# Two groups of columns per cycle, with one stretch of 64-row tiles, in a Fourier mixing layer

## The chip, the cores and the metric

The kernel runs on one core of one Trainium2 chip. The metric is the device time of one execution in microseconds (us). The kernel before takes 5095.11 us, the median of three runs (5094.22 to 5102.17).

## What is computed

x is 4 images of 128 x 128 pixels with 768 channels in 8 blocks of 96. All in float32:

```
xf = rfft2(x, axes=(1, 2), norm='ortho')          # 128 x 65 frequencies, complex
o1 = relu(xf @ w1[block] + b1)                    # complex product, relu on both parts
o2 = o1 @ w2[block] + b2                          # complex product
o  = softshrink(o2, 0.01)                         # on both parts
out = irfft2(o, s=(128, 128), norm='ortho') + x
```

## The kernel before

**Units and stages.** One unit is one image and one block of 96 channels; there are 32 units, and x of two units lies in SBUF (`xs[0]`, `xs[1]`, index `par`). For a unit n, TensorE (PE) does stage A (transform along the width, 24 groups of 4 rows, L760), the layers, and the inverse (E, L849, and F, L859 to L861). Two of the 24 A groups of unit n+1 (`AHEAD`) come between the layers and the inverse of unit n, the others behind the inverse. ScalarE (ACT) and VectorE (DVE) copy A's results into `spectrum` (U), split E's results into two parts, and add F's results to x.

**The layers.** They go through 17 groups s of up to four column frequencies (`GROUPS`; group 2, `REAL`, has two, the last has three). Stage B is the transform along the height's channels times w1: `stage_b_whole` (L778, 128-row tiles) and `stage_b_halved` (L790), where two tiles of 64 rows, y = 0 and y = 1, lie in the upper and the lower half of PE's rows. Stage C (L807) is the transform along the height. Stage D is the product with w2: `stage_d_outer` (L822, 128 rows) and `stage_d_middle` (L832, 64-row tiles). One full fp32 matmul shows as two records, so a full group has 8 records in each of L778, L790, L822 and L832 and 12 in L807.

**Who does what between them.** ACT gathers a group's columns out of U into `whole` (L493, L494) and `halved` (L495, L496), which have two buffers each, `s % 2`. DVE copies B's result to `mixed` (L655). ACT applies bias and relu to C's outer tiles, giving `hidden` (L530, L533), and DVE to the middle tile, giving `middle` (L668). DVE writes b2 into D's banks ahead (the seed, L678). ACT computes `excess` (L524) and DVE the softshrink (L663). B is in PSUM banks 0 and 1, C in 2 and 3, D in 4, 5 for even groups and 6, 7 for odd ones. Group REAL goes through `real_kw` and the flip, two matmuls at L839 and L840, copied to U by ACT (L536).

**Order.** Each engine runs its own list in program order; semaphores are the only ties. PE's cycle s (L864) is: whole of s, outer and middle of s-2, halved of s, C of s-1. So the 64-row tiles of middle and halved form one stretch per group. DVE's cycle (L645) is: mixed(s), shrink(s-2), middle(s-1), seed(s), then in cycles 2 to 9 one `unfold_step` of the unit before (two for each of four pieces of x, each about a quarter of the rows), and in cycles 10 to 15 one `prepare_step` (sign changes of the next unit's weights, L611 and L615; the first waits for these weights).

**x and the weights.** When both unfold steps of a piece are done, SyncE's queue (SP) stores the piece (L392). Its order is: store piece 0, load the next unit's weights (L367), store piece 1, load piece 0 of the unit after next (L387), store 2, load 1, store 3, load 2, load 3. GpSimd (POOL) folds each loaded piece in two steps (L439 to L445), and stage A waits for the fold of its piece.

Of the kernel before, what the change touches and what calls it, by code (L numbers as in the profile page):

```python
# [1 line left out]

# [7 lines left out]
ALU = mybir.AluOpType  # L10
# [17 lines left out]
REAL = 2  # L28

# [130 lines left out]
def fourier_mlp(nc, x, w1, b1, w2, b2, dft, out):  # L160
    with ExitStack() as ctx:
# [60 lines left out]
        def banks_b(s):  # L222

            return 6 if s == 1 else 0
# [15 lines left out]
        bank_c = bank(2).rearrange("p (y i h) -> p y i h", y=2, i=2)  # L240
        middle_c = bank(3, SIZE, 2 * SIZE).rearrange("p (i h) -> p i h", i=2)
# [51 lines left out]
        b_done, b_copied = sem("b_done"), sem("b_copied")  # L293
# [175 lines left out]
        def _(act):  # L469
            def gather(s):  # L470
                w, h, first = whole[s % 2], halved[s % 2], GROUPS[s][0]
                if s == REAL:
                    re, im = (U[:, :, j:j + 2].rearrange("p s k -> p k s") for j in (2, SIZE + 2))
                    act.activation(w[0:BLOCK, :, :, 0], re[0:BLOCK], ACT.Copy)
                    act.activation(w[BLOCK:SIZE, :, :, 0], im[HALF:BLOCK], ACT.Copy).then_inc(whole_gathered, 1)
                    act.activation(h[0:HALF, :, 0], im[0:HALF, 0], ACT.Copy)
                    act.activation(h[HALF:SIZE, :, 0], im[0:HALF, 1], ACT.Copy).then_inc(halved_gathered, 1)
                    return
# [5 lines left out]
                if GROUPS[s][3] is None:  # L484
# [3 lines left out]
                    act.activation(w[BLOCK:SIZE, 1, :, 0], U[HALF:BLOCK, :, j + 5], ACT.Copy).then_inc(whole_gathered, 1)  # L488
                    act.activation(h[0:HALF], U[0:HALF, :, j + 2:j + 4], ACT.Copy)
# [3 lines left out]
                act.activation(w[0:BLOCK], parts[0:BLOCK, 0], ACT.Copy)  # L493
                act.activation(w[BLOCK:SIZE], parts[HALF:BLOCK, 1], ACT.Copy).then_inc(whole_gathered, 1)  # L494
# [3 lines left out]
            def forward(n):  # L498
                for at in A_ACT:
# [4 lines left out]
                    act.activation(third, src[BLOCK:], ACT.Copy).then_inc(act_copied, 1)  # L504
            def layers(m, par, n):
# [4 lines left out]
                gather(0)  # L510
                act.wait_ge(w_loaded[par], (m + 1) * W_LOADS * 16)
                for s in range(NS + 2):
                    if s + 1 < NS:
                        if s >= 1:
                            act.wait_ge(b_done, n * NS + s)
                        gather(s + 1)

                    for stage in ("sums", "tiles") if s < NS else ("tiles", "sums"):
                        if stage == "sums" and s >= 2:
                            t = s - 2  # L520
                            act.wait_ge(d_done, n * NS + (t + 1))
                            if t >= 1:
                                act.wait_ge(shrunk, n * NS + t)
                            act.activation(excess[:, :, 0:rows_d(t)], parts_d(t), ACT.Relu,  # L524
                                           bias=over[:, 0:1]).then_inc(excess_done, 1)
                        if stage == "tiles" and 1 <= s <= NS:
                            t = s - 1
                            act.wait_ge(c_done, n * NS + (t + 1))
                            tiles = hidden[t % 2]
                            act.activation(tiles[:, 0, 0:pairs(t)], bank_c[:, 0, 0:pairs(t)], ACT.Relu,  # L530
                                           bias=b1t[par][:, 0:1]).then_inc(relu_done, 1)
                            k = pairs(t) if None not in GROUPS[t] else 1
                            act.activation(tiles[:, 1, 0:k], bank_c[:, 1, 0:k], ACT.Relu,  # L533
                                           bias=b1t[par][:, 2:3]).then_inc(relu_done, 1)
# [27 lines left out]
        def _(dve):  # L562
# [54 lines left out]
            def forward(n):  # L617
# [26 lines left out]
                dve.tensor_copy(halved[0][HALF:SIZE, slice(*INNER)], parts[0:HALF, 1, 1]).then_inc(first_halved, 1)  # L644
            def layers(m, par, n, first, last):  # L645
                for s in range(NS + 2):
                    if s < NS:
                        k = pairs(s)
                        dve.wait_ge(b_done, n * NS + (s + 1))
                        if s == 1:  # L650
                            for i in range(2):
                                flat = mixed[s % 2][:, i].rearrange("p y (r o) -> p y r o", r=2)
                                copied = dve.tensor_copy(flat, both_b(s, i))
                        else:
                            copied = dve.tensor_copy(mixed[s % 2][:, 0:k], both_b(s)[:, 0:k])  # L655
                        copied.then_inc(b_copied, 1)
                    for stage in ("sums", "tiles") if s < NS else ("tiles", "sums"):
                        if stage == "sums" and s >= 2:
                            t, rows = s - 2, rows_d(s - 2)
                            j = 2 + 2 * GROUPS[t][0]  # L660
                            dst = real_kw[:, :, :] if t == REAL else U[:, 0:BLOCK, j:j + rows]
                            dve.wait_ge(excess_done, n * NS + (t + 1))
                            dve.scalar_tensor_tensor(dst, parts_d(t), LAMBDA, excess[:, :, 0:rows], op0=ALU.add,  # L663
                                                     op1=ALU.min).then_inc(shrunk, 1)
                        if stage == "tiles" and 1 <= s <= NS:
                            t = s - 1
                            dve.wait_ge(c_done, n * NS + (t + 1))
                            dve.tensor_scalar(middle[t % 2][:, 0:pairs(t)], middle_c[:, 0:pairs(t)], b1t[par][:, 1:2], 0.0,  # L668
                                              ALU.add, ALU.max).then_inc(middle_done, 1)
                    if s < NS:  # L670


                        k = rows_d(s) // 2
                        if s == 1:
                            dve.wait_ge(b_copied, n * NS + 2)
                        elif s >= 2:
                            dve.wait_ge(shrunk, n * NS + (s - 1))
                        dve.tensor_copy(bank_d(s).rearrange("p (k r) c -> p k r c", r=2)[:, 0:k],  # L678
                                        b2_rows[par][:, :, :].unsqueeze(1).broadcast_to([SIZE, k, 2, BLOCK])).then_inc(seeded, 1)

                    if 2 <= s < 2 + 2 * NP and not first:
                        unfold_step(n - 1, 1 - par, s - 2)

                    if 2 + 2 * NP <= s < 2 + 2 * NP + W_SIGNS and not last:
                        prepare_step(m + par, 1 - par, s - 2 - 2 * NP)
# [244 lines left out]
```

## Time and profile before

| what | value |
|---|---|
| time of the profiled execution | 5094.22 us, span 5094.2 us |
| median of three | 5095.11 us |
| PE busy | 4981.3 us, 98% |
| DVE busy | 3816.7 us, 75% |
| ACT busy | 2996.3 us, 59% |
| POOL busy | 1436.3 us, 28% |
| mean granted TensorE clock | 0.993 |
| DMA | 430.24 MB, mean 84 GB/s |

The span runs from the first to the last instruction. Matmul records overlap, since the next one starts while the last one's results are still leaving the array; what one block of matmuls costs is therefore read from the start of its first record to the start of the next block's first record. A unit takes 5094.2 / 32 = 159 us.

### The profile page before, as it was taken

To read this page: it belongs to the slowest core of one execution; us is meant where nothing else is said; L and a number is where in the kernel's file an instruction comes from. 1 tells how busy PE (TensorE), PEld (TensorE's weight loads), DVE (VectorE), ACT (ScalarE), POOL (GpSimd) and SP (SyncE) were. 2 spreads that over 40 slices of the span, in tenths; PEclk is the share of its full clock that TensorE was granted. 3 is DMA by queue.
4 is the path that set the end of the run, shared out by engine and by line. 5 is a ranking of instruction groups with operands and counts; after the bars stand their busy time and mean duration, and the time that the engine had idled before them with its cause. 6 is when DMAs were issued, how large, how long until landed. Compare 5 with 4: busy or idle time off the path is not lost.

```text
span 5094.2 us, 113221 instructions
## 1 busy us (share of the span) xinstructions
PE 4981.3 (98%) x40000; PEld 4673.3 (92%) x40000; DVE 3816.7 (75%) x6159; ACT 2996.3 (59%) x5409; POOL 1436.3 (28%) x905
## 2 busy tenths in 40 slices
PE   6999999999999999999999999999999999999997
PEld 6999999999999999999999999999999999999996
DVE  5777777777777777777777777777777777777876
ACT  4555655556655566555566555665556655556653
POOL 3033223332123332233321333312333123332220
PEclk8999999999999999999999999999999999999998
DMA  5044423444323443234442344432344323444233
GB/s 114 12 94 105 98 59 69 91 105 105 68 57 87 105 105 87 56 81 94 105 105 52 70 90 105 106 70 62 79 105 106 86 61 78 92 105 105 61 73 72
DMA packets 1699712, 430.24 MB, mean 84 GB/s; under 512 B 1698848, under 2 KB 1698976, under 8 KB 1699104
## 3 DMA queue, kind: packets, MB, share of 16 engines
q1 hardware_dynamic: 1696768, 421.83, 37.5%
q8 instruction: 346, 5.67, 0.5%
q14 instruction: 262, 2.15, 0.1%
q10 hardware_dynamic: 2336, 0.59, 0.1%
HBM read 220.84 MB, written 201.33 MB: 83 GB/s over the span
## 4 chain that ended last, share of the span: by engine, by line
PE 96%; DVE 2%; issue 1%; SPq 1%; ACT 0%; DMA 0%; DVEq 0%; ACTq 0%
PE psum L807 15%; PE psum L778 14%; PE psum L822 14%; PE psum L760 13%; PE psum L849 13%; PE psum L832 9%; PE psum L790 7%; PE psum L859 3%; PE psum L860 3%; PE psum L861 3%; DVE mixed L655 1%; SPq L387 1%; DVE spectrum L628 0%; PE psum L840 0%; PE psum L839 0%
## 5 line engine op out<-in xcount | busy, mean ns | idle before, releaser
L655 DVE COPY mixed<-psum 128x768 f32<-128x768 f32 (+1 forms) x512 | 477.4, 932 | 700.0 <-PE psum L790 700.0
L541 ACT ACTIVATE sums_high<-psum 128x512 fp32r<-128x512 f32 x768 | 459.2, 599 | 731.3 <-PE psum L849 731.2
L807 PEld LDWEIGHTS psum<-mats,mixed 128*128 128x128 f32 x6272 | 744.0, 191 | 121.2 <-issue 113.1
L807 PE MATMUL psum<-mats,mixed 128*128 128x128 f32 x6272 | 841.8, 283 | 0.0
L778 PE MATMUL psum<-w_whole,whole 128*128 128x192 f32 x4160 | 782.3, 330 | 40.9 <-ACT whole L482 11.4
L822 PE MATMUL psum<-w2t,hidden 128*128 128x192 f32 x4160 | 771.7, 328 | 0.0
L849 PE MATMUL psum<-mats,spectrum 128*128 128x128 f32 x6144 | 743.7, 275 | 3.1 <-DVE spectrum L663 1.6
L760 PE MATMUL psum<-mats,x 128*128 128x128 f32 x6144 | 704.9, 277 | 33.6 <-DVE x L582 17.8
L760 PEld LDWEIGHTS psum<-mats,x 128*128 128x128 f32 x6144 | 696.0, 193 | 40.9 <-issue 23.0
L778 PEld LDWEIGHTS psum<-w_whole,whole 128*128 128x128 f32 x4160 | 673.3, 197 | 60.6 <-issue 33.7
L849 PEld LDWEIGHTS psum<-mats,spectrum 128*128 128x128 f32 x6144 | 714.5, 192 | 4.1 <-DVE sums_low L701 2.0
L701 DVE TENSOR_TENSOR sums_low<-psum,sums_high 128x512 fp32r<-128x512 f32 x768 | 530.4, 691 | 248.8 <-ACT sums_high L541 248.7
L822 PEld LDWEIGHTS psum<-w2t,hidden 128*128 128x128 f32 x4160 | 685.9, 190 | 13.4 <-issue 7.2
L524 ACT ACTIVATE excess<-psum,over 128x768 f32<-128x768 f32 (+1 forms) x544 | 481.8, 886 | 332.8 <-PE psum L832 329.9
L530 ACT ACTIVATE hidden<-psum,b1t 128x256 f32<-128x256 f32 (+1 forms) x544 | 254.6, 468 | 688.8 <-PE psum L807 688.8
L453 POOL TENSOR_TENSOR x<-x,half 128x3072 f32<-128x3072 f32 x32 | 169.8, 5307 | 1450.0 <-DVE halved L644 1450.0
L663 DVE SCALAR_TENSOR_TENSOR spectrum<-psum,excess 128x768 f32<-128x768 f32 (+1 forms) x512 | 480.8, 939 | 118.7 <-ACT excess L524 113.0
L678 DVE COPY psum<-b_rows 128x768 f32<-128x768 f32 (+1 forms) x544 | 504.0, 926 | 0.0
L436 POOL TENSOR_TENSOR x<-x 128x192 f32<-128x192 f32 x31 | 15.7, 505 | 1700.4 <-DMA x<-x 1700.4
L832 PE MATMUL psum<-w2t,middle 64*128 64x192 f32 x4160 | 490.3, 350 | 0.0
L859 PE MATMUL psum<-sums_high,iw_high 128*128 128x260 f32 (+1 forms) x1536 | 461.8, 301 | 0.0
L445 POOL TENSOR_TENSOR x<-x,doubled 128x640 f32<-128x640 f32 (+1 forms) x248 | 443.4, 1788 | 17.0
(76 smaller groups left out, 7800.7 us busy)
## 6 DMA issues: line engine op xcount, KB each, us to landing
x<-x SPq DMA_DIRECT2D x736, 192.0 KB, 2.9
out<-x SPq DMA_DIRECT2D x736, 192.0 KB, 2.5
x<-x SPq DMA_DIRECT2D x736, 64.0 KB, 2.6
out<-x SPq DMA_DIRECT2D x736, 64.0 KB, 2.2
x<-x SPq DMA_DIRECT2D x32, 144.0 KB, 2.7
out<-x SPq DMA_DIRECT2D x32, 144.0 KB, 2.3
w2t<-L_conv_w SPq DMA_DIRECT2D x124, 36.0 KB, 1.8
x<-x SPq DMA_DIRECT2D x64, 48.0 KB, 2.4
```

The source lines that it names most:

```text
L524: act.activation(excess[:, :, 0:rows_d(t)], parts_d(t), ACT.Relu, bias=over[:, 0:1]).then_inc(excess_done, 1)
L655: copied = dve.tensor_copy(mixed[s % 2][:, 0:k], both_b(s)[:, 0:k])
L663: dve.scalar_tensor_tensor(dst, parts_d(t), LAMBDA, excess[:, :, 0:rows], op0=ALU.add, op1=ALU.min).then_inc(shrunk, 1)
L678: dve.tensor_copy(bank_d(s).rearrange("p (k r) c -> p k r c", r=2)[:, 0:k], b2_rows[par][:, :, :].unsqueeze(1).broadcast_to([SIZE, k, 2, B ...
L701: dve.tensor_tensor(sums_low[:, q % RING], bank_e(q), sums_high[:, q % RING], ALU.subtract).then_inc(low_copied, 1)
L760: last = pe.matmul(bank_a(at)[:, i * SIZE:(i + 1) * SIZE], xs[par][:, j, :], mat(FW_EVEN if g[0] < NP else FW_ODD), start=i == 0, stop=Tru ...
L778: pe.matmul(bank_b(s, k), whole[s % 2][:, k // 2, :, k % 2], w1_whole[par][:, :, :].rearrange("p r o -> p (r o)"), start=k % 2 == 0, stop= ...
L807: last = pe.matmul(out[tile], flat[:, tile * SIZE:(tile + 1) * SIZE], mat(FH), start=True, stop=True)
L822: pe.matmul(sums_d(s, k), hidden[s % 2][:, k // 2, k % 2], w2_tile(par, slice(0, SIZE), 2 * (k // 2)), start=False, stop=False, skip_group ...
L832: last = pe.matmul(sums_d(s, i + 2 * y), middle[s % 2][rows, i], w2_tile(par, rows, 1), start=False, stop=True, skip_group_check=True)
L849: last = pe.matmul(bank_e(q)[:, :, i], U[:, q * CHUNK + i, 4:], mat(IH_FIRST if q * CHUNK < THIRD else IH), start=True, stop=True)
L859: pe.matmul(out, iw_high[:, j], high, start=True, stop=False)
```

## The change

PE takes groups in pairs (`PAIRED`: (0, 1), (2, 3), ..., (14, 15), (16)). For a pair (e, o) and the pair before it (e', o'), the cycle is: halved(e), middle(e'), halved(o), middle(o'), whole(e), outer(e'), whole(o), outer(o'), C(e), C(o). All 64-row tiles of the four stages form one stretch. Since halved now comes before whole, halved opens the accumulation (`start`) and whole closes it; in D, middle now opens and outer closes. B and C of an odd group are in banks 2 and 3, of an even one in 0 and 1, and C writes into the banks that B had; so halved(s) waits for the relus and the middle of group s-2. The semaphore `b_done` becomes two, `whole_read` and `halved_read`. For the first pair the two wholes come first, then the two halved, then both C. At the end of the layers one A group of the next unit comes before middle(16), and the flip comes last, followed by the second A group. ACT and DVE follow in the same pairs. DVE's unfold steps are one per pair (cycles 1 to 8), the sign steps two per pair (cycles 5 to 7), between mixed(e) and shrink(e').

```diff
+PAIRED = [tuple(range(s, min(s + 2, NS))) for s in range(0, NS, 2)]
...
-            return 6 if s == 1 else 0
+            return 6 if s == 1 else 2 * (s % 2)
...
-        bank_c = bank(2).rearrange("p (y i h) -> p y i h", y=2, i=2)
-        middle_c = bank(3, SIZE, 2 * SIZE).rearrange("p (i h) -> p i h", i=2)
+        def bank_c(s):
+            return bank(2 * (s % 2)).rearrange("p (y i h) -> p y i h", y=2, i=2)
+
+        def middle_c(s):
+            return bank(2 * (s % 2) + 1, SIZE, 2 * SIZE).rearrange("p (i h) -> p i h", i=2)
...
+                gather_whole(1)
+                gather_halved(1)
+                for j, pair in enumerate(PAIRED):
+                    e, o = pair[0], pair[-1]
+                    for s in pair:
+                        if s + 2 < NS:
+                            if j == 0 and s == e:
+                                act.wait_ge(whole_read, n * NS + (s + 1))
+                                gather_whole(s + 2)
+                            act.wait_ge(halved_read, n * NS + (s + 1))
+                            gather_halved(s + 2)
+                    if j > 0:
+                        if o != e:
+                            act.wait_ge(whole_read, n * NS + (o - 1))
+                            gather_whole(o)
+                        exceed(n, PAIRED[j - 1][0])
+                        if e + 2 < NS:
+                            act.wait_ge(whole_read, n * NS + (e + 1))
+                            gather_whole(e + 2)
+                        exceed(n, PAIRED[j - 1][1])
+                    for s in pair:
+                        rectify(par, n, s)
+                exceed(n, NS - 1)
...
+                for j, pair in enumerate(PAIRED):
+                    e, o = pair[0], pair[-1]
+                    mix(n, e)
+                    for k in range(2 * (j - 5), 2 * (j - 5) + 2):
+                        if 0 <= k < W_SIGNS and not last:
+                            prepare_step(m + par, 1 - par, k)
+                    if j > 0:
+                        shrink(n, PAIRED[j - 1][0])
+                    if o != e:
+                        mix(n, o)
+                    seed(par, n, e)
+                    rectify_middle(par, n, e)
+                    if j > 0:
+                        shrink(n, PAIRED[j - 1][1])
+                    if o != e:
+                        rectify_middle(par, n, o)
+                        seed(par, n, o)
+                    if 1 <= j <= 2 * NP and not first:
+                        unfold_step(n - 1, 1 - par, j - 1)
+                shrink(n, NS - 1)
...
             def stage_c(n, s):
                 pe.wait_ge(b_copied, n * NS + (s + 1))
-                if s == 0:
+                if s == 1:
 
                     pe.wait_ge(f_late_added, n * LATE)
-                if s >= 1:
-                    pe.wait_ge(relu_done, n * (2 * NS) + 2 * s)
-                    pe.wait_ge(middle_done, n * NS + s)
...
+            def layers(par, n, ahead):
+                for s in PAIRED[0]:
+                    stage_b_whole(par, n, s, True)
+                for s in PAIRED[0]:
+                    stage_b_halved(par, n, s, False)
+                for s in PAIRED[0]:
+                    stage_c(n, s)
+                for before, pair in zip(PAIRED, PAIRED[1:]):
+                    for s, t in zip_longest(pair, before):
+                        if s is not None:
+                            stage_b_halved(par, n, s, True)
+                        stage_d_middle(par, n, t)
+                    for s, t in zip_longest(pair, before):
+                        if s is not None:
+                            stage_b_whole(par, n, s, False)
+                        stage_d_outer(par, n, t)
+                    for s in pair:
+                        stage_c(n, s)
+                if ahead:
+                    stage_a(*ahead, 0, 1)
+                stage_d_middle(par, n, NS - 1)
+                stage_d_outer(par, n, NS - 1)
+                flip(n)
+                if ahead:
+                    stage_a(*ahead, 1, AHEAD)
```

PE's list in the middle of the layers of the kernel before, from whole of one group on. `w_whole,whole` is the B whole stage, `w2t,hidden` the outer and `w2t,middle` the middle stage of D, `w_halved,halved` the B halved stage, `mats,mixed` stage C; REGISTER_ALU rows prepare a wait.

```order
L775 REGISTER_ALU
L778 MATMUL psum<-w_whole,whole 128x192 x4
L817 REGISTER_ALU
L822 MATMUL psum<-w2t,hidden 128x2x96 x2
L821 REGISTER_ALU
L822 MATMUL psum<-w2t,hidden 128x2x96 x2
L832 MATMUL psum<-w2t,middle 128x2x96 x4
L785 REGISTER_ALU
L790 MATMUL psum<-w_halved,halved 128x192 x4
L807 MATMUL psum<-mats,mixed 128x128 x6
```

The 64-row rows, L832 and L790, stand together, once per group. The same place in the changed kernel, from halved(e) on:

```order
L839 MATMUL psum<-w_halved,halved 128x192 x4
L870 MATMUL psum<-w2t,middle 128x2x96 x4
L830 REGISTER_ALU
L833 REGISTER_ALU
L839 MATMUL psum<-w_halved,halved 128x192 x4
L870 MATMUL psum<-w2t,middle 128x2x96 x4
L819 REGISTER_ALU
L822 MATMUL psum<-w_whole,whole 128x192 x4
L876 MATMUL psum<-w2t,hidden 128x2x96 x4
L819 REGISTER_ALU
L822 MATMUL psum<-w_whole,whole 128x192 x4
L876 MATMUL psum<-w2t,hidden 128x2x96 x4
```

Halved and middle alternate four times in one stretch, then whole and outer four times; the row behind these is `mats,mixed` x12, the C of both groups. In both kernels every stage has the same number of matmuls per group.

DVE's list of the kernel before, around the first sign steps (L611). What is in brackets is what the row waits for.

```order
L678 COPY psum<-b_rows 128x8x96 [waits shrunk]
L611 TENSOR_SCALAR w_whole<-w_whole 32x96 [waits w_loaded1]
L655 COPY mixed<-psum 128x768 [waits b_done]
L663 SCALAR_TENSOR_TENSOR spectrum<-psum,excess 128x96x8 [waits excess_done]
L668 TENSOR_SCALAR middle<-psum,b1t 128x256 [waits c_done]
L678 COPY psum<-b_rows 128x8x96 [waits shrunk]
L611 TENSOR_SCALAR w_halved<-w_halved 128x96
```

And of the changed kernel, cycle 5 from mixed(e) to the seed of o and on to the next mixed(e):

```order
L686 COPY mixed<-psum 128x768 [waits halved_read,whole_read]
L643 TENSOR_SCALAR w_whole<-w_whole 32x96 [waits w_loaded1]
L643 TENSOR_SCALAR w_halved<-w_halved 128x96
L694 SCALAR_TENSOR_TENSOR spectrum<-psum,excess 128x96x8 [waits excess_done]
L686 COPY mixed<-psum 128x768 [waits halved_read,whole_read]
L708 COPY psum<-b_rows 128x8x96 [waits shrunk]
L699 TENSOR_SCALAR middle<-psum,b1t 128x256 [waits c_done]
L694 SCALAR_TENSOR_TENSOR spectrum<-psum,excess 128x96x8 [waits excess_done]
L699 TENSOR_SCALAR middle<-psum,b1t 128x256 [waits c_done]
L708 COPY psum<-b_rows 128x8x96 [waits shrunk]
L686 COPY mixed<-psum 128x768 [waits halved_read,whole_read]
```

Both first sign steps, with the wait for the weights, now stand between mixed(e) and shrink(e'), ahead of mixed(o). The unfold step of this cycle stands behind its last seed and is a row of its own in a unit other than the first.

## Rows read from the trace of the kernel before

**Rows 1.** The page's busy times and shares of the span.

```profile
PE 4981.3 (98%) x40000; PEld 4673.3 (92%) x40000; DVE 3816.7 (75%) x6159; ACT 2996.3 (59%) x5409; POOL 1436.3 (28%) x905
```

**Rows 2.** Idle time of the weight loads (PEld) before a line: us, times, longest.

```profile
PEld psum L832 <- issue: 122.4, 544, 0.2
PEld psum L807 <- issue: 113.1, 516, 0.3
...
PEld psum L790 <- issue: 14.6, 64, 0.4
```

**Rows 3.** Timeline, a steady cycle, PE: start us, us, what.

```profile
2608.12 1.60 PE L807 MATMUL psum<-mats,mixed 128*128 128x128 f32 x12
...
2609.56 1.47 PE L778 MATMUL psum<-w_whole,whole 128*128 128x192 f32 x8
...
2610.87 1.46 PE L822 MATMUL psum<-w2t,hidden 128*128 128x192 f32 x8
...
2612.26 0.92 PE L832 MATMUL psum<-w2t,middle 64*128 64x192 f32 x8
...
2613.02 0.82 PE L790 MATMUL psum<-w_halved,halved 64*128 64x192 f32 x8
```

**Rows 4.** Timeline, PE at the head of a unit.

```profile
2577.09 1.57 PE L778 MATMUL psum<-w_whole,whole 128*128 128x192 f32 x8 [1.66 <-ACT whole L494]
2578.59 0.93 PE L790 MATMUL psum<-w_halved,halved 64*128 64x192 f32 x8
2579.45 1.58 PE L778 MATMUL psum<-w_whole,whole 128*128 128x192 f32 x8
...
2592.30 0.94 PE L807 MATMUL psum<-mats,mixed 128*128 128x128 f32 x6
2593.51 1.57 PE L778 MATMUL psum<-w_whole,whole 128*128 128x192 f32 x8 [0.27 <-DVE mixed L655]
```

**Rows 5.** Timeline, DVE and ACT in the steady cycle.

```profile
2607.59 0.90 ACT L524 ACTIVATE excess<-psum,over 128x768 f32<-128x768 f32 x1 [0.48 <-PE psum L832]
...
2608.24 0.96 DVE L655 COPY mixed<-psum 128x768 f32<-128x768 f32 x1 [0.91 <-PE psum L790]
2609.11 0.95 DVE L663 SCALAR_TENSOR_TENSOR spectrum<-psum,excess 128x768 f32<-128x768 f32 x1
...
2609.76 0.47 ACT L530 ACTIVATE hidden<-psum,b1t 128x256 f32<-128x256 f32 x1 [1.27 <-PE psum L807]
...
2610.37 0.95 DVE L678 COPY psum<-b_rows 128x768 f32<-128x768 f32 x1
2610.49 0.66 ACT L493 ACTIVATE whole<-spectrum 96x512 f32<-96x512 f32 x1
...
2611.23 1.75 DVE L598 TENSOR_TENSOR x<-x 128x1536 f32<-128x1536 f32 x1
```

**Rows 6.** Timeline of DVE: unfold step 1, and one w2t step.

```profile
2595.38 1.62 DVE L603 SCALAR_TENSOR_TENSOR x<-x 128x1408 f32<-128x1408 f32 x1
...
2656.50 1.40 DVE L615 TENSOR_SCALAR w2t<-w2t 32x96 f32<-32x96 f32 x1
```

**Rows 7.** Timeline of SP's queue: the store of piece 1.

```profile
2620.49 6.88 SPq L392 DMA_DIRECT2D out<-x  x12
```

**Rows 8.** The page's DMA issues: KB each, us from issue to landing.

```profile
w2t<-L_conv_w SPq DMA_DIRECT2D x124, 36.0 KB, 1.8
```

**Rows 9.** Instructions of L615 (w2t signs): ns minimum, median, maximum.

```profile
L615 DVE TENSOR_SCALAR w2t<-w2t x128: 191/538/1767, 67.4 to 4852.3; 32x96 f32<-32x96 f32 x64, 64x96 f32<-64x96 f32 x64
```

**Rows 10.** Timeline of POOL: folds of the x pieces.

```profile
2637.49 0.50 POOL L436 TENSOR_TENSOR x<-x 128x192 f32<-128x192 f32 x1 [55.91 <-DMA x<-x]
...
2646.33 1.80 POOL L445 TENSOR_TENSOR x<-x,doubled 128x768 f32<-128x768 f32 x1
...
2656.03 1.81 POOL L445 TENSOR_TENSOR x<-x,doubled 128x768 f32<-128x768 f32 x1
```

**Rows 11.** Timeline, PE's first inverse matmuls after the layers.

```profile
2674.51 3.75 PE L849 MATMUL psum<-mats,spectrum 128*128 128x128 f32 x32
```

More of the change, by code:

```diff
@@ L469, in _, with gather_whole @@
         def _(act):
-            def gather(s):
-                w, h, first = whole[s % 2], halved[s % 2], GROUPS[s][0]
+            def gather_whole(s):
+                w, first = whole[s % 2], GROUPS[s][0]
                 if s == REAL:
@@ L504, in forward, with rectify, exceed @@
                     act.activation(third, src[BLOCK:], ACT.Copy).then_inc(act_copied, 1)
+            def rectify(par, n, t):
+                act.wait_ge(c_done, n * NS + (t + 1))
+                tiles = hidden[t % 2]
+                act.activation(tiles[:, 0, 0:pairs(t)], bank_c(t)[:, 0, 0:pairs(t)], ACT.Relu,
+                               bias=b1t[par][:, 0:1]).then_inc(relu_done, 1)
+                k = pairs(t) if None not in GROUPS[t] else 1
+                act.activation(tiles[:, 1, 0:k], bank_c(t)[:, 1, 0:k], ACT.Relu,
+                               bias=b1t[par][:, 2:3]).then_inc(relu_done, 1)
+            def exceed(n, t):
+                act.wait_ge(d_done, n * NS + (t + 1))
+                if t >= 1:
+                    act.wait_ge(shrunk, n * NS + t)
+                act.activation(excess[:, :, 0:rows_d(t)], parts_d(t), ACT.Relu,
+                               bias=over[:, 0:1]).then_inc(excess_done, 1)
             def layers(m, par, n):
@@ L509, in layers @@
                 act.wait_ge(dve_copied, (n + 1) * len(A_DVE))
-                gather(0)
+                gather_whole(0)
                 act.wait_ge(w_loaded[par], (m + 1) * W_LOADS * 16)
-                for s in range(NS + 2):
-                    if s + 1 < NS:
-                        if s >= 1:
[L515 to L534, printed above, removed]
@@ L644, in forward @@
                 dve.tensor_copy(halved[0][HALF:SIZE, slice(*INNER)], parts[0:HALF, 1, 1]).then_inc(first_halved, 1)
-            def layers(m, par, n, first, last):
[L646 to L685, printed above, removed]
@@ new lines, in mix @@
+            def mix(n, s):
+                k = pairs(s)
+                dve.wait_ge(whole_read, n * NS + (s + 1))
+                dve.wait_ge(halved_read, n * NS + (s + 1))
+                if s == 1:
+                    for i in range(2):
+                        flat = mixed[s % 2][:, i].rearrange("p y (r o) -> p y r o", r=2)
+                        copied = dve.tensor_copy(flat, both_b(s, i))
+                else:
+                    copied = dve.tensor_copy(mixed[s % 2][:, 0:k], both_b(s)[:, 0:k])
+                copied.then_inc(b_copied, 1)
@@ new lines, in shrink, with rectify_middle @@
+            def shrink(n, t):
+                rows = rows_d(t)
+                j = 2 + 2 * GROUPS[t][0]
+                dst = real_kw[:, :, :] if t == REAL else U[:, 0:BLOCK, j:j + rows]
+                dve.wait_ge(excess_done, n * NS + (t + 1))
+                dve.scalar_tensor_tensor(dst, parts_d(t), LAMBDA, excess[:, :, 0:rows], op0=ALU.add,
+                                         op1=ALU.min).then_inc(shrunk, 1)
+            def rectify_middle(par, n, t):
+                dve.wait_ge(c_done, n * NS + (t + 1))
+                dve.tensor_scalar(middle[t % 2][:, 0:pairs(t)], middle_c(t)[:, 0:pairs(t)], b1t[par][:, 1:2], 0.0,
+                                  ALU.add, ALU.max).then_inc(middle_done, 1)
@@ L771, in stage_b_whole, with stage_b_halved @@
                     pe.wait_ge(early_gathered, (n + 1) * 3)
[L772 to L774 removed]
                 pe.wait_ge(whole_gathered, n * NS + (s + 1))
                 for k in columns(s):
[L778 to L781 removed]
+                    last = pe.matmul(bank_b(s, k), whole[s % 2][:, k // 2, :, k % 2], w1_whole[par][:, :, :].rearrange("p r o -> p (r o)"),
+                                     start=opens and k % 2 == 0, stop=not opens, skip_group_check=True)
+                last.then_inc(whole_read, 1)
+            def stage_b_halved(par, n, s, opens):
                 if s == 0:
```

83 lines of the change are left out of this document (40 added, 43 removed).

## The prediction

> **What bounds the kernel now.** I read the page's shares first: PE is busy for 98% of the span, DVE for 75% [rows 1]. So work that comes off another engine gives nothing, and a change pays if PE does its work in less time or waits less. The number of matmuls is the same in both kernels. What can change is the time between them, so I went to the idle time of the weight loads. There 608 gaps (544 + 64) of about 0.22 us stand ahead of a stretch of 64-row tiles, and 516 more ahead of L807 where such a stretch has just ended; they are put down to "issue", so no semaphore ended them [rows 2]. 608 is 19 stretches in each of the 32 units. This is the only large PE loss that I see; what waits there are on semaphores inside the layers come to a few tenths of a us per unit, like the 0.27 in [rows 4].
>
> **Price of one stretch.** A record is half an fp32 matmul, so a full group has 8 records for each of its four 192-column stages. In the steady cycle L832 and L790, 16 records of 64 rows, run from 2612.26 to 2613.76: 1.50 us [rows 3] (the end is the start of the next L807, 5.64 us after the one shown). At the head of a unit L790 runs alone, 8 records from 2578.59 to 2579.45: 0.86 us [rows 4]. So 8 more records in a stretch cost 0.64 us and the stretch itself a fixed 0.22. Outside, L778 takes 1.31 us when 128-row work stands on both sides, and 1.50 when a stretch stands on either side [rows 3, 4]; L822 ahead of a stretch takes 1.39 instead of 1.31. So the entry costs 0.08 more and the exit 0.11 more. Together 0.22 + 0.08 + 0.11 = 0.41 us per stretch.
>
> The Trainium skill, TensorEngine Tiling (Array Packing), Key Properties, says that changing the tiling mode drains TensorE, which puts the cost on the change of mode and not on the number of tiles, as [rows 2] do; it gives no duration.
>
> **The change, part by part.**
> 1. PE order. Before, a unit has a stretch in each of its 17 groups and two more at the end: 19. After, one for groups 0 and 1, eight for the cycles that follow (the last with group 16 alone), one for the second layer of group 16: 10. Nine are gone: 9 x 0.41 = 3.7 us per unit. From below: only the 0.22 gap is saved, 2.0 us; from above, entry and exit gaps both count besides the borders, 9 x 0.6 = 5.4. I take 3.7, since it comes from starts alone.
>
> 2. Steady cycle, t = 0 at the first 64-row record. PE: halved(e) 0, middle(e') 0.75, halved(o) 1.4, middle(o') 2.0, whole(e) 2.8, outer(e') 4.2, whole(o) 5.5, outer(o') 6.8, C(e) 8.1, C(o) 9.5, next cycle 10.9 (two old cycles are 11.3). A consumer starts 0.2 us after the start of PE's next block [rows 3, 5], or 0.12 at a switch. DVE (durations from [rows 5]): mixed(e) 4.4 to 5.3. ACT: excess(e') 5.7 to 6.6. DVE: shrink(e') 6.65 to 7.6, mixed(o) 7.6 to 8.5. C(o) needs it at 9.4: 0.9 us spare. C(e) has 2.7 spare. DVE: seed(e) to 9.4, middle(e) 9.7 to 10.1, shrink(o') 10.1 to 11.0, middle(o) 11.0 to 11.5, seed(o) to 12.4, an unfold step to 14.1, that is 3.2 of the next cycle, whose mixed comes at 4.4. PE's middle(o') at 2.0 (12.9) needs seed(o) at 1.5: 0.4 spare. ACT: two relus end 0.96 into the cycle, halved(e+2) to 1.9, halved(o+2) from 2.2 to 3.1 (0.9 a pair), whole(o) to 4.5, needed at 5.5; whole(e+2) 6.6 to 8.0; excess(o') 8.3 to 9.2, before C(e)'s relu at 9.7. So no wait in the steady cycle: 0. The bound is the 0.4 on seed(o): if everything of DVE is 0.8 later than I have it, each of 7 cycles loses 0.4, 2.8 us per unit.
>
> 3. Head of the unit. C(0) now waits for mixed(0), which starts at the end of the whole stretch's first half; PE reaches C(0) at 4.3 and has it at 4.7: a loss of 0.4. In the cycle of groups 4 and 5 the short middle(REAL) pulls PE ahead of seed(3): 0.4 again. The old loss ahead of group 4's L778 goes: it starts at 2593.51, 1.21 us after the six records of L807 began [rows 4], which by the pace of the other L807 (1.44 for twelve, an exit in them [rows 3]) should take 0.78: 0.4, and I add a tenth for the wait at the flip, so 0.5 back. By the sum the first steady cycle (groups 4 and 5) begins 16.7 us after the first L778, the next ones at 27.0, 37.9, 48.8, 59.6, 70.5 and 81.4, and C(16) ends at 88.2.
>
> 4. Weight signs. prepare_step 0 waits for the next unit's weights. Now its place is cycle 5, after mixed(e): 48.8 + 5.3 = 54.1. The weights are issued behind the store of piece 0, which waits for unfold step 1. Before, that step ended at 2597.00 the store that follows the last weight load was issued at 2620.49, and such a load lands after 1.8: some 25.1 us [rows 6 to 8]. Now step 1 ends at 27.0 + 3.1 = 30.1, so the weights are there at 55.2. DVE waits 1.1 us and two short steps follow until 55.7, where shrink(e') would have begun at 55.5. Loss 0.1 us; every us that the weights are later costs PE a us from there on, less some 0.7 of cover.
>
> 5. Signs beside POOL. The w2t steps take between 0.19 and 1.77 us [rows 9], and the slow ones lie beside POOL's fold (the one at 2656.50 took 1.40, L445 of POOL at work since 2656.03 [rows 6, 10]). Before they stood last in the cycle, with idle DVE behind them. Now two stand ahead of shrink and mixed(o). The fold of piece 0 starts 17.0 us after the store of piece 1 is issued (2620.49 to 2637.49 [rows 7, 10]); that store now comes at 53.8, so the fold runs 70.9 to 81.5 and meets only the pair in cycle 7. Two by 1.1: mixed(o) ends at 9.4, loss 0.1; two by 1.77: loss 1.3. I take 0.2.
>
> 6. The x round trip. Two unfold steps per two cycles instead of two per two groups make it later; DMA has idle shares for that, so what counts is when PE needs a piece. Piece 0 folded at 81.5; the first group of the next A now stands ahead of group 16's second layer, at 88.2: 6.7 us spare, so 0. The last piece is unfolded at about 91.5, and 14 us of stores, 14 of loads and two folds of 10.6 (one of them behind the other on POOL, 2637.49 to 2648.13 [rows 10]) end near 130; PE wants it only after the inverse, in the last 15 us of a unit of 159 (5094.2 / 32): 0.
>
> 7. End of the unit. From C(16): A group 0.9, middle 0.7, outer 1.1, flip 1.2, A group 1.1: PE reaches the inverse at 4.9. excess(16) ends at 3.8 and shrink(16) at 4.6, after unfold step 7 (1.6 to 3.4). The flip's copy ends at 4.6. Loss 0, with 0.3 spare.
>
> A rule that speaks against items 5 and 7: the Trainium skill, SBUF — State Buffer, Who interferes with whom, says that VectorE's second port pair is shared with GpSimd as an exclusive lock, and the one that comes second stands still for the whole instruction. The spread from 0.19 to 1.77 in [rows 9] agrees with that; that the unfold steps (two SBUF inputs) would be held in the same way no row here shows, since none of them meets a fold in the unit that I read. It is a rival below.
>
> **Sum.** 3.7 + 0.5 - 0.4 - 0.4 - 0.1 - 0.2 = 3.1 us per unit. Times 32: 99 us. As a check, both kernels' layers with their two A groups: 97.4 us before (2577.09 to 2674.51 [rows 4, 11]), and 88.2 + 4.9 + 0.3 = 93.4 by the schedule, a gain of 4.0. I go near the sum made of differences. The profiled execution's span is 5094.2 and its time 5094.22; the median of three is 5095.11. 5095 - 99 = 4996.
>
> **Rivals.**
> A. DVE and POOL hold each other. Every unfold step that meets a fold (steps 5 to 7 may) comes up to 1.8 us late, the length of one POOL op, and the sign pair of cycle 7 takes 3.5. In cycle 7: mixed(e) ends at 5.9, signs at 9.4, shrink 10.3, mixed(o) 11.2 against 9.4: 1.8 lost; at the end shrink(16) at 6.4 against 4.9: 1.5 lost. 3.1 - 3.3 + 0.3 = about 0: 5090; half of it gives 5045. For: [rows 9]. Against: POOL is idle in most of the cycles, and the fold of piece 1 would start at about 90, when step 7 is already under way.
> B. The gap is not the stretch's but is paid again between tiles of the two stages when they alternate four times: then only the borders are saved, 9 x 0.19, less the new waits of 1.1, with 0.5 back: 1.1 per unit, 5060. Against: L790 follows L832 without a gap of its own in [rows 3].
> C. Slower: the weights. If they land 5 us later than item 4 has it (their 26 transfers share the queues with the stores), every unit loses 4.3 at mixed(o) of cycle 5, more than the 3.1 gained: 5094 + 38 = 5132. It decides from 3.8 us of lateness. Against: nothing else is in the queues at that time, as before.
> D. The change does not do what it says, since each pair's chain over DVE is too long and PE waits in each cycle: 0.8 us of lateness makes about 0.4 x 7 = 2.8: 5085.
>
> **How the numbers follow.** Forecast (4970 to 5025) 0.66; A 0.14, of which three quarters still faster; B 0.05; C 0.07; D 0.08, half of it faster by enough. A measurement of this kernel can tell 0.2%, 10 us, from no change. Faster: 0.66 + 0.10 + 0.05 + 0.04 = 0.85. Same: 0.04 + 0.02 = 0.06. Slower: 0.09. The range from 4965 to 5065 takes in the upper bound of item 1 in part (5.4 would give 4945, which I find unlikely), half of A, and B; it leaves out C and D.
>
> **What would show it.** The weight loads' "issue" gaps fall to 320 ahead of 64-row tiles; PE's cycle of two full groups takes 10.9 us; the waits on PE name mixed (C(0), C(o) in cycles 5 and 7) with some tenths each. It is wrong if such waits come in every cycle, if the first A group waits for POOL, if the sign steps wait for a DMA for more than 2 us, or if 32 records of 64 rows take much more than 2.8 us.

## The result and the profile after

| | median of the runs | interval of the ratio to before |
|---|---|---|
| before | 5097.65 us (4 runs) | |
| changed | 5048.9 us (4 runs, 5046.55 to 5061.01) | 0.9907 (0.9895 to 0.9919) |

The changed kernel is 49 us faster by the medians, or 0.9%; the spans of the two profiled executions, 5094.2 and 5046.4 us, differ by 48. The forecast was a gain of 99 us, to 4996. The time lies inside the wide range (4965 to 5065) and outside the narrow one around the forecast (4970 to 5025); the gain is just under half of what was forecast. The page's first line of the changed kernel, against [rows 1]:

```profile
PE 4878.2 (97%) x40000; PEld 4718.3 (93%) x40000; DVE 3829.9 (76%) x6159; ACT 3005.9 (60%) x5409; POOL 1511.3 (30%) x905
```

PE is 103 us less busy, which is close to the forecast gain, yet the span fell by 48 only: the other half has turned into waiting. Cycle 5 of one unit (groups 10 and 11, and the second layer of 8 and 9) shows both. PE of the changed kernel, start, duration, what, in brackets the idle time ahead of it and what ended it, against [rows 3]:

```profile
2596.75 0.93 PE L839 MATMUL psum<-w_halved,halved 64*128 64x192 f32 x8
2597.51 0.82 PE L870 MATMUL psum<-w2t,middle 64*128 64x192 f32 x8
2598.16 0.82 PE L839 MATMUL psum<-w_halved,halved 64*128 64x192 f32 x8
2598.81 0.82 PE L870 MATMUL psum<-w2t,middle 64*128 64x192 f32 x8
2599.56 1.58 PE L822 MATMUL psum<-w_whole,whole 128*128 128x192 f32 x8
2600.97 1.46 PE L876 MATMUL psum<-w2t,hidden 128*128 128x192 f32 x8
2602.27 1.46 PE L822 MATMUL psum<-w_whole,whole 128*128 128x192 f32 x8
2603.57 1.46 PE L876 MATMUL psum<-w2t,hidden 128*128 128x192 f32 x8
2604.87 1.50 PE L853 MATMUL psum<-mats,mixed 128*128 128x128 f32 x12
2608.05 1.60 PE L853 MATMUL psum<-mats,mixed 128*128 128x128 f32 x12 [1.67 <-DVE mixed L686]
2609.58 0.93 PE L839 MATMUL psum<-w_halved,halved 64*128 64x192 f32 x8
```

The eight blocks up to the first L853 come within 0.06 us of the times forecast (0.75, 1.4, 2.0, 2.8, 4.2, 5.5, 6.8, 8.1 after the cycle's start). Then the C of the odd group should follow at 9.5, which is 2606.25, and comes at 2608.05. The cycle takes 12.83 us where 10.9 was forecast. Here is what DVE does meanwhile:

```profile
2601.17 0.96 DVE L686 COPY mixed<-psum 128x768 f32<-128x768 f32 x1 [1.30 <-PE psum L822]
2605.81 0.20 DVE L643 TENSOR_SCALAR w_whole<-w_whole 32x96 f32<-32x96 f32 x1 [3.68 <-DMA b_rows<-L_conv_b]
2606.05 0.21 DVE L643 TENSOR_SCALAR w_halved<-w_halved 128x96 f32<-128x96 f32 x1
2606.18 0.95 DVE L694 SCALAR_TENSOR_TENSOR spectrum<-psum,excess 128x768 f32<-128x768 f32 x1
2607.04 0.95 DVE L686 COPY mixed<-psum 128x768 f32<-128x768 f32 x1
```

mixed(e) ends at 2602.1, and the first sign step waits 3.68 us for the last of the weight loads; shrink(e') and mixed(o), on which PE waits, stand behind it. The waits by pair of engines, us in total, times, longest, first DVE, then PE:

```profile
DVE mixed L686 <- PE psum L822: 308.1, 252, 3.0
...
DVE w_whole L643 <- DMA b_rows<-L_conv_b: 93.8, 30, 4.3
```


```profile
PE psum L853 <- DVE mixed L686: 57.0, 73, 2.3
...
PE psum L870 <- DVE psum L708: 3.2, 12, 0.3
```

DVE waits for the weights in 30 units, 3.1 us each on average. PE waits for mixed 73 times. By the starts in the trace 32 of these are C(0) at the head of a unit (15.3 us), 29 are in cycle 5 (33.7 us) and 12 in cycle 7 (8.0 us). The 12 waits for a seed (L708) are in cycle 8.

The loads of the weights of the changed kernel, as SP's queue issues them:

```profile
2578.27 8.56 SPq L398 DMA_DIRECT2D out<-x  x14
...
2602.56 0.40 SPq L373 DMA_DIRECT2D b_rows<-L_conv_b  x1
2603.22 6.88 SPq L398 DMA_DIRECT2D out<-x  x12
```

Unfold step 1 ends 0.2 us before 2578.27. Before, the store behind the weights comes at 2620.49, 23.5 us after the step [rows 6, 7]; here it comes 25.2 us after it. This is a difference between two single units and not between the kernels: over the 30 units that load weights this stretch takes 24.6 us on average in both kernels (23.4 to 26.2 before, 23.6 to 25.7 after). The 14 stores take 8.56 us to issue here. And the last load, b2's rows, takes longer to land than the w2t loads of [rows 8]. DMA issues of that stretch, KB each and us to landing, changed and then before:

```profile
b_rows<-L_conv_b SPq DMA_DIRECT2D x1, 96.0 KB, 3.2
```


```profile
b_rows<-L_conv_b SPq DMA_DIRECT2D x1, 96.0 KB, 3.1
```

Over the 30 units, from the end of unfold step 1 to the landing of the last load, it is 27.2 us on average in both kernels. The unit that the forecast was read from is the fastest of the 30 before, with 25.95.

I worked out a table from the starts in the traces, as means over the 32 units, with the same cuts in each kernel. The layers run from the first L822 (L778 before) to the first E matmul; the last column is the rest of a unit (E, F and A), up to the next unit's first L822. Cycle j is the one that takes pair j of `PAIRED`, from its first halved on, and the head is what comes before cycle 1.

| us per unit | head | cycle 1 | 2 | 3, 4 | 5 | 6 | 7 | 8 and end | layers | rest |
|---|---|---|---|---|---|---|---|---|---|---|
| before | | | | | | | | | 97.56 | 58.98 |
| changed | 7.91 | 9.28 | 9.94 | 10.89 | 12.19 | 10.89 | 11.24 | 12.66 | 95.90 | 59.14 |
| weights_first | 7.85 | 9.28 | 9.95 | 10.89 | 10.89 | 10.89 | 10.89 | 12.53 | 94.07 | 59.16 |
| bias_rows_first | 7.95 | 9.28 | 9.95 | 10.89 | 11.05 | 10.89 | 10.89 | 12.53 | 94.33 | 59.17 |
| middle_apart | 7.91 | 9.68 | 10.35 | 11.29 | 11.29 | 11.29 | 11.29 | 12.71 | 97.09 | 59.17 |
| flip_early | 7.90 | 9.28 | 9.95 | 10.89 | 10.89 | 10.89 | 10.89 | 13.23 | 94.82 | 59.15 |

The changed kernel's layers gain 1.67 us (97.56 to 95.90, before rounding) and the rest loses 0.16: 1.5 x 32 = 48 us.

### The profile page after: what moved, and what is told of

Same layout as the page of the kernel before. It is cut to its first block, busy times and chain, and to the rows that moved or that the text cites. A ratio compares the mean times of both kernels' runs of the same rounds, so it can differ in the third digit from the quotient of the medians.

```text
span 5046.4 us, 113165 instructions
## 1 busy us (share of the span) xinstructions
PE 4878.2 (97%) x40000; PEld 4718.3 (93%) x40000; DVE 3829.9 (76%) x6159; ACT 3005.9 (60%) x5409; POOL 1511.3 (30%) x905
## 4 chain that ended last, share of the span: by engine, by line
PE 74%; SPq 12%; DVE 7%; issue 4%; DMA 2%; ACT 0%; DVEq 0%; ACTq 0%
PE psum L807 13%; PE psum L892 13%; PE psum L822 10%; PE psum L853 9%; PE psum L876 8%; SPq L373 8%; PE psum L839 5%; PE psum L870 5%; SPq L398 4%; PE psum L902 3%; PE psum L903 3%; PE psum L904 3%; DMA b_rows<-L_conv_b 2%; DVE mixed L686 2%; DVE spectrum L694 1%
## 5 line engine op out<-in xcount | busy, mean ns | idle before, releaser
L822 PE MATMUL psum<-w_whole,whole 128*128 128x192 f32 x4160 | 797.5, 335 | 33.4 <-ACT whole L496 12.0
L853 PE MATMUL psum<-mats,mixed 128*128 128x128 f32 x6272 | 761.0, 276 | 57.0 <-DVE mixed L686 57.0
L853 PEld LDWEIGHTS psum<-mats,mixed 128*128 128x128 f32 x6272 | 739.0, 192 | 74.1 <-DVE mixed L686 74.0
L822 PEld LDWEIGHTS psum<-w_whole,whole 128*128 128x128 f32 x4160 | 685.4, 197 | 97.1 <-issue 70.9
L445 POOL TENSOR_TENSOR doubled<-x 128x640 f32<-128x640 f32 (+1 forms) x248 | 373.6, 1506 | 497.0 <-DMA x<-x 483.5
L708 DVE COPY psum<-b_rows 128x768 f32<-128x768 f32 (+1 forms) x544 | 504.9, 928 | 1.1
L446 POOL TENSOR_TENSOR x<-x 128x640 f32<-128x640 f32 (+1 forms) x248 | 495.4, 1998 | 0.0
L839 PE MATMUL psum<-w_halved,halved 64*128 64x192 f32 x4160 | 462.6, 339 | 0.0
L870 PE MATMUL psum<-w2t,middle 64*128 64x192 f32 x4160 | 449.3, 326 | 4.1 <-DVE psum L708 3.2
```

The costliest lines, as they stand in the source:

```text
L822: last = pe.matmul(bank_b(s, k), whole[s % 2][:, k // 2, :, k % 2], w1_whole[par][:, :, :].rearrange("p r o -> p (r o)"), start=opens and ...
L839: last = pe.matmul(bank_b(s, i + 2 * y), halved[s % 2][rows, :, i], w1_halved[par][rows, :, :].rearrange("p r o -> p (r o)"), start=opens ...
L853: last = pe.matmul(out[tile], flat[:, tile * SIZE:(tile + 1) * SIZE], mat(FH), start=True, stop=True)
L870: pe.matmul(sums_d(s, i + 2 * y), middle[s % 2][rows, i], w2_tile(par, rows, 1), start=False, stop=False, skip_group_check=True)
```

## The experiments

Theory W: the missing half is DVE's wait for the weights in cycle 5 and what follows from it. Theory P, the rival: DVE and POOL hold each other, and the weights' wait only covers that. The runs below were taken in other sets than the changed kernel's; the kernel before took 5098.39 and 5098.16 us in these sets against 5097.65, so the times can be compared.

**weights_first.** On SP's queue the weight loads go ahead of the store of piece 0:

```diff
                 sp.wait_ge(unfolded, (m * 2 + par) * NP + (p + 1))
+                if weights:
+                    load_w(sp, m + 1, par)
                 for tile, image in transfers(xs[par], pixels(out, m, par), p):
...
                         if p < NP:
-                            store_piece(m, par, p)
+                            store_piece(m, par, p, weights=p == 0)
...
-                        if p == 0:
-                            load_w(sp, m + 1, par)
```

> The changed kernel, with the next unit's weight loads issued ahead of the store of piece 0 instead of behind it, at the same wait. Theory W: the time lost against the forecast is DVE's wait for the weights in cycle 5. The weights then come about 8.5 us sooner (the 14 stores took 8.56 us to issue), DVE's 93.8 us of waiting for b_rows goes to 0, cycle 5 falls from a mean of 12.2 us to 10.9, and the kernel gains 1.3 x 32 = 41 us: 5048 - 41 = 5007. Theory P: DVE and POOL holding each other is what costs, and the weights wait only covers it; then cycle 5 stays near 12 and the time is within 10 us of 5048.

Measured: 4991.16 us (4989.55 to 4993.91), ratio to before 0.9788 (0.977 to 0.9805), 58 us below the changed kernel. PE's waits:

```profile
PE psum L853 <- DVE mixed L686: 15.3, 32, 0.5
```

The wait for mixed is left 32 times, once per unit at the head, and DVE has no wait for weights any more. Cycle 5 takes 10.89 in every unit. It gains more than the 41 of theory W, since cycle 7's loss (0.35) and the end's (0.12) go as well, though the sign steps of cycle 7 stand where they stood. W holds, and P falls for cycle 5. In cycle 7 it was P's mechanism that made the sign steps slow, but only in a kernel in which cycle 5 came late: the pair there takes up to 3.1 us in the changed kernel and at most 1.6 here.

**signs_last.** The sign steps go behind the unfold step:

```diff
                     mix(n, e)
-                    for k in range(2 * (j - 5), 2 * (j - 5) + 2):
-                        if 0 <= k < W_SIGNS and not last:
-                            prepare_step(m + par, 1 - par, k)
...
                         unfold_step(n - 1, 1 - par, j - 1)
+                    for k in range(2 * (j - 5), 2 * (j - 5) + 2):
+                        if 0 <= k < W_SIGNS and not last:
+                            prepare_step(m + par, 1 - par, k)
```

> The changed kernel, with the two sign steps of cycles 5 to 7 behind the unfold step, last in the cycle, instead of between mixed(e) and shrink(e'). Theory W: both losses of the signs go, 1.3 us in cycle 5 and 0.35 in cycle 7, since the weights (55 to 58 us into a unit) are there at 62 and since slow signs then delay only a mixed(e) that has spare time: 1.65 x 32 = 53 us, 4995. Theory P: the loss of cycle 7 goes and the unfold steps' stays; no more than 11 us, 5037.

Measured: 4992.78 us (4992.46 to 4996.51), ratio 0.9789 (0.9771 to 0.9806), as W has it. The weights are as late as in the changed kernel (57.4 us into a unit on average, 57.3 there), but DVE comes to the sign steps later than that and has no wait for weights left, and neither shrink nor mixed(o) of the cycle stands behind them.

**bias_rows_first.** b2's rows are loaded first of the weights instead of last:

```diff
+            put(b2_rows[par][:, :, :], b2[:, blk].partition_broadcast(SIZE))
             put(w1_whole[par][0:BLOCK], w1[:, blk].rearrange("r i o -> i r o"))
...
-            put(b2_rows[par][:, :, :], b2[:, blk].partition_broadcast(SIZE))
```

> The changed kernel, with the load of b2's rows as the first of the 26 weight loads instead of the last. That load (96 KB, written to all partitions) lands 3.1 to 3.2 us after its issue, the w2t loads after 1.8; the forecast had reckoned with 1.8 for the last one. Theory W: the weights are complete about 1.3 us sooner, every us of lateness costs PE a us, so cycle 5 falls from 12.2 to about 11.0 and the kernel gains 1.2 to 1.4 x 32: 5005, near weights_first. Rival, that the issue of the stores and loads is what comes late and the last landing does not matter: no gain, 5048.

Measured: 4996.63 us (4996.11 to 4998.82), ratio 0.9801 (0.9784 to 0.9817). DVE's wait:

```profile
DVE w_whole L643 <- DMA b1t<-L_conv_b: 52.3, 30, 2.7
```

52.3 us instead of 93.8, or 1.7 us per unit instead of 3.1, and cycle 5 falls by 1.14 us. The last load is still issued 23.9 us after unfold step 1, as in the changed kernel (24.0), but it is now one of b1's and lands 1.9 us later and not 3.2. Unit by unit the two kernels give one rule: what cycle 5 takes beyond 10.89 is DVE's wait less 1.74 us, and nothing when the wait is shorter (in the changed kernel waits of 1.89, 2.33 and 4.30 cost 0.14, 0.59 and 2.56). The 1.3 us of landing time were enough to cost most of the missing gain. The time is 8 us below the expected 5005, since the losses of cycle 7 and of the end go here too.

**both_mends.** weights_first and signs_last together.

> weights_first and signs_last together. Theory W: either of them alone has taken the wait off PE, so nothing is left to gain: 4991, within 5. If each removed a part of its own, below 4985.

Measured: 4990.09 us (4987.06 to 4991.72), ratio 0.9786 (0.977 to 0.9803). It is the fastest by its median, but not apart from weights_first: the two mend the same loss.

**middle_apart.** One more stretch per cycle, from signs_last:

```diff
                             stage_b_halved(par, n, s, True)
-                        stage_d_middle(par, n, t)
+                        if t != before[-1]:
+                            stage_d_middle(par, n, t)
...
                         if s is not None:
                             stage_b_whole(par, n, s, False)
+                        if t != before[-1]:
+                            stage_d_middle(par, n, before[-1])
                         stage_d_outer(par, n, t)
```

> signs_last, with middle(o') taken out of the stretch and put behind whole(e), ahead of outer(e'): the same matmuls and waits, one more stretch of 64-row tiles in each of eight cycles. Theory of the 0.41 us: 8 x 32 x 0.41 = 105 us more than signs_last. If only the gap of the weight loads counts, 8 x 32 x 0.22 = 56. If the cost lay between tiles that alternate inside a stretch and not at its borders, about 0.

Measured: 5086.7 us (5082.76 to 5088.48), ratio 0.9973 (0.9962 to 0.9985), 94 us more than signs_last. PE, one cycle:

```profile
2602.75 0.93 PE L839 MATMUL psum<-w_halved,halved 64*128 64x192 f32 x8
2603.51 0.81 PE L870 MATMUL psum<-w2t,middle 64*128 64x192 f32 x8
2604.16 0.82 PE L839 MATMUL psum<-w_halved,halved 64*128 64x192 f32 x8
2604.91 1.58 PE L822 MATMUL psum<-w_whole,whole 128*128 128x192 f32 x8
2606.41 0.92 PE L870 MATMUL psum<-w2t,middle 64*128 64x192 f32 x8
2607.26 1.57 PE L876 MATMUL psum<-w2t,hidden 128*128 128x192 f32 x8
...
2614.04 0.93 PE L839 MATMUL psum<-w_halved,halved 64*128 64x192 f32 x8
```

The cycle is 11.29 us and not 10.89: 0.40 for one stretch, the forecast's 0.41. In cycle 8 only 0.18 shows; why is open. 7 x 0.40 + 0.18 = 3.0 us per unit, or 95, where 105 was expected. The price of a stretch is shown, and that it lies at the borders and is more than the 0.22 us gap of the weight loads.

**flip_early.** From weights_first, the flip ahead of outer(16), with a wait for its relus, and ACT's copy of it ahead of excess(16):

```diff
-                exceed(n, NS - 1)
                 act.wait_ge(flip_done, n + 1)
...
+                exceed(n, NS - 1)
...
                 stage_d_middle(par, n, NS - 1)
-                stage_d_outer(par, n, NS - 1)
+                pe.wait_ge(relu_done, n * (2 * NS) + 2 * NS)
                 flip(n)
+                stage_d_outer(par, n, NS - 1)
```

> weights_first, with the flip ahead of outer(16) instead of behind it, and its copy ahead of excess(16) on ACT. If the last place of the flip is worth something: outer(16) then ends 1.34 us later, excess(16), shrink(16) and the start of the inverse stand behind it, 0.2 + 0.77 + 0.05 + 0.75 + 0.1 = 1.85 us, and only the second A group (1.1 us) covers that; PE waits 0.7 us per unit, 32 x 0.7 = 22 us more than weights_first: 5013. If it is worth nothing: 4991.

Measured: 5014.51 us (5011.69 to 5017.18), ratio 0.9836 (0.9819 to 0.9852), 23 us more. The inverse now waits for the last shrink in each unit:

```profile
PE psum L892 <- DVE spectrum L694: 18.4, 32, 1.6
```

So the flip's last place is worth 0.7 us per unit in this order.

**unfold_early.** Two unfold steps in each of cycles 1 to 4, from signs_last:

```diff
                     mix(n, e)
+                    if 1 <= j <= NP and not first:
+                        unfold_step(n - 1, 1 - par, 2 * j - 2)
...
-                        unfold_step(n - 1, 1 - par, j - 1)
+                        unfold_step(n - 1, 1 - par, 2 * j - 1)
```

> signs_last, with two unfold steps in each of cycles 1 to 4 (one behind mixed(e), one last) instead of one in each of cycles 1 to 8. The x round trip and the weights then come up to 40 us sooner and POOL folds in cycles 5 to 8, beside the signs only. Theory W: the remaining losses outside the layers (0.16 us per unit) and at the end (0.12) come from the late x traffic, and go: 9 us below signs_last, if the unfold step behind mixed(e) (1.75 us against 1.3 idle) stays inside the 0.9 us that mixed(o) has to spare. Rival: it does not, and each of four cycles loses up to 0.4: 32 x 1.6 = 51 us more.

Measured: 4991.67 us (4988.88 to 4992.96), ratio 0.9785 (0.9767 to 0.9802): no change from signs_last's 4992.78 that can be told. POOL's first fold starts 62.3 us into a unit on average, against 72.2 in signs_last and 60.4 in the unit read before [rows 4, 10]. Yet the rest of a unit takes 59.18 us there, so the 0.16 us does not come from late x traffic, and this expectation was wrong. The rival's loss does not come either.

## Why the prediction was right and wrong

- **Stretches (item 1).** Right: nine at 0.41. The steady cycle was forecast at 10.9 and is 10.89, and middle_apart pays 0.40 for one more stretch. The gaps ahead of L822, where a stretch ends, against [rows 2]:

```profile
PEld psum L822 <- issue: 70.9, 261, 10.4
...
PEld psum L839 <- issue: 7.2, 32, 0.4
PEld psum L876 <- issue: 7.2, 32, 0.2
```

There are 261 "issue" gaps instead of 516. The gaps at the entry are hardly listed any more (32 at L839), where the forecast's sign was a fall to 320. So the price of 0.41 held, but not its division into a gap at the entry and two borders; why the entry from L853 shows no gap is open.
- **Steady cycle (item 2).** Right: no wait in cycles 3, 4 and 6. Rivals B and D fall.
- **Head (item 3).** Right in kind, and in its sum by luck: C(0) waits 0.5 us for mixed(0) (32 times, 15.3 us), forecast 0.4. Cycle 2 was forecast at 10.3 and takes 9.94, without the loss of 0.4. But it begins 17.0 us into the unit shown (7.74 and 9.28; the mean head of 7.91 holds three slow units) and not at 16.7. The two misses cancel, and cycle 3 begins at 27.0, as forecast.
- **Weights (item 4).** This step failed, by its size. The mechanism, the place and the cover were right: I had the weights at 55.2 us into a unit, DVE waiting 1.1 us and PE losing 0.1, and from there one us per us of lateness, less 0.7 of cover. In the unit shown the wait begins at 54.1, as forecast, and the weights are there at 57.8; on average they land at 57.3, 2 us late. The mean wait is 3.1 us, and cycle 5 loses 1.30 (2.0 less 0.7): 42 us in all, where 3 were forecast. My sign of being wrong, a wait for a DMA of more than 2 us at the sign steps, came true.

  The forecast took 25.1 us from unfold step 1 to the last landing, and the mean is 27.2. Two terms of this sum were too small. First, the last load lands after 3.2 us on average, not 1.8, which the trace of before could have told me, had I read the row of the load that comes last and not of the one with the most bytes in all; this is 1.4 of the 2 us, and bias_rows_first shows that it alone takes away 1.14 of the 1.30. Second, the last load is issued 23.9 us after the step on average in both kernels, where 25.1 less 1.8 leaves 23.3; the unit that I read has 22.8 and is the fastest of the 30. This is the other 0.6 us. (The rows that item 4 names, 23.5 and 1.8, add up to 25.3.)

  Rival C was this mechanism, with a lateness of 5 us; it came with 2, short of the 3.8 from which the change would have lost.
- **Signs beside POOL (item 5).** Forecast 0.2, found 0.35 in cycle 7, and it goes with the lateness of cycle 5. The sign steps are slow when a POOL instruction runs as they arrive (below), and when they arrive shifts with the cycle. Half of rival A would have given 5045, close to the time measured, so the time alone would have pointed to A. Its lock exists, but it costs PE nothing once the weights are in time.
- **x round trip and end (items 6, 7).** Right: no wait for POOL beyond the first unit's. By durations the end is longer than I had it (12.5 us for cycle 8 and end against 6.8 + 4.9; the parts of item 7 add up to 5.0), which the sum by differences does not use. The end also loses 0.12 us per unit that was not forecast, PE's wait for a seed in 12 units; it comes in the units that lose in cycle 7.
- **Not in the forecast.** The rest of a unit takes 0.16 us more, 5 us in all. Of these, 3.6 us fall on one unit in four, and 1.2 on the unit before it. One of the former:

```profile
2644.30 0.53 ACT L567 ACTIVATE spectrum<-psum 128x192 f32<-128x192 f32 x1 [0.58 <-PE psum L883]
2647.22 1.57 ACT L573 ACTIVATE sums_high<-psum 128x512 fp32r<-128x512 f32 x3 [2.38 <-PE psum L892]
```


```profile
2645.22 2.84 PE L892 MATMUL psum<-mats,spectrum 128*128 128x128 f32 x24
2648.60 1.16 PE L892 MATMUL psum<-mats,spectrum 128*128 128x128 f32 x8 [0.54 <-DVE sums_low L748]
```

ACT's copy of the first E result starts 2.0 us after E has begun, where it is 1.1 us in the other units. These are the units in which ACT's loop turns back, between the flip's copy and this copy. Before, the flip's copy ends 0.8 us ahead of E, and three of the six such units have a late copy (1.6 to 1.9 us); in the changed kernel it ends 0.4 us ahead, and all six have one (1.9 to 2.4). That it is the turn of the loop fits the one-in-four pattern and was not tested.

The losses add up. The 94.07 + 59.16 of weights_first are 3.3 us per unit below before, and the forecast without its 0.3 for items 4 and 5 was 3.4. From there 1.30 in cycle 5, 0.35 in cycle 7, 0.12 at the end and 0.06 at the head lead to the layers of the changed kernel. With item 4 at its measured 1.3 the forecast's sum would have been 1.9 us per unit, 61 us; what remains to the 48 measured is 0.15 in cycle 7, 0.12 at the end and 0.16 in the rest.

## What to carry to other kernels

When the time of an engine is lost at the borders between two kinds of work, measure one border from starts on both sides and count the borders; that number held here to 0.01 us per cycle. Before moving an instruction that waits for a DMA ahead of others on its engine, work out when the last of these transfers lands, from that transfer's own row, and over all units and not in one: here the unit read was the fastest of 30, 1.2 us below the mean. Where such an instruction can stand last in its cycle, put it there: then its lateness costs nothing.

## What the runs showed of the hardware

A change between 128-row and 64-row tiles and back costs 0.40 us of PE, while alternating two stages of 64-row tiles inside a stretch costs nothing that shows. The first two blocks of cycle 5 above, halved and middle, run from 2596.75 to 2598.33, 1.58 us for 16 records. Sixteen of halved alone, at the head of the same unit, take as long:

```profile
2550.82 1.58 PE L839 MATMUL psum<-w_halved,halved 64*128 64x192 f32 x16
```

DVE and POOL do hold each other for whole instructions. DVE of the changed kernel, then POOL, in the same unit:

```profile
2621.84 2.23 DVE L635 SCALAR_TENSOR_TENSOR x<-x 128x1536 f32<-128x1536 f32 x1
...
2625.88 3.02 DVE L647 TENSOR_SCALAR w2t<-w2t 32x96 f32<-32x96 f32 x2
...
2634.04 1.75 DVE L630 TENSOR_TENSOR x<-x 128x1536 f32<-128x1536 f32 x1
...
2641.48 2.49 DVE L635 SCALAR_TENSOR_TENSOR x<-x 128x1536 f32<-128x1536 f32 x1
```


```profile
2621.20 1.25 POOL L445 TENSOR_TENSOR doubled<-x 128x640 f32<-128x640 f32 x1
2622.41 3.05 POOL L446 TENSOR_TENSOR x<-x 128x640 f32<-128x640 f32 x1
...
2625.76 1.54 POOL L451 TENSOR_TENSOR x<-x,doubled 128x640 f32<-128x640 f32 x1
2627.37 1.47 POOL L445 TENSOR_TENSOR doubled<-x 128x768 f32<-128x768 f32 x1
...
2640.89 1.47 POOL L445 TENSOR_TENSOR doubled<-x 128x768 f32<-128x768 f32 x1 [8.38 <-DMA x<-x]
2642.31 3.33 POOL L446 TENSOR_TENSOR x<-x 128x768 f32<-128x768 f32 x1
...
2649.03 1.84 POOL L446 TENSOR_TENSOR x<-x 128x768 f32<-128x768 f32 x1
```

The unfold step takes 1.75 us alone (L635 at 2598.12 in this unit; before, none of the 256 unfold steps takes more than 1.76), and 2.23 and 2.49 beside a fold. Both times a POOL instruction was running when it began, and it ended 1.6 us after that instruction's end (2622.45 and 2642.36). POOL's add, L446, takes 3.05 and 3.33 instead of 1.53 and 1.84 when an unfold step has begun before it. The two w2t steps at 2625.88 together took 3.02 us, up to the end of the second of the two POOL instructions that ran meanwhile (2628.84), while in one unit of weights_first the same two took 0.71. The Trainium skill, SBUF — State Buffer, Who interferes with whom, has this rule, also for VectorE instructions with two SBUF inputs, which no row of before had shown; here it is seen.
